# Cross-attention, second phase: steps taken in groups of two, and the next batch's context transposed two groups at a time

## The reference

```
q = (layernorm(x) @ w_q)          # [2, 16 heads, 256, 64]
k = (ctx @ w_k); v = (ctx @ w_v)  # [2, 16 heads, 4096, 64]
attn = softmax(q @ k^T * 64**-0.5)
x = x + (attn @ v) @ w_o
```

## Time and profile before

| | |
|---|---|
| median of 3 runs | 1409.45 us (1409.3 to 1412.59) |
| the profiled execution | 1410.72 us, span 1409.0 us |
| busy | PE 1292.7 us (92%), PEld 1004.9, DVE 868.2, ACT 882.1, POOL 407.6 |
| cross-attention | ends near 1140 us; self-attention and feed-forward take the rest |
| granted TensorE clock, mean | 0.967 of full speed |

### The profile page before, as it was taken

How to read it: one execution, slowest core, us unless ns; L and a number is a source line. 1 busy time by engine, 2 the same in 40 slices (tenths; PEclk the granted TensorE clock), 3 DMA queues, 4 the chain that set the end, 5 groups by cost and what they waited for, 6 DMA issues and landing times. The chain is left out here.

```text
span 1409.0 us, 22447 instructions
## 1 busy us (share of the span) xinstructions
PE 1292.7 (92%) x8447; PEld 1004.9 (71%) x8447; DVE 868.2 (62%) x1121; ACT 882.1 (63%) x1543; POOL 407.6 (29%) x373
## 2 busy tenths in 40 slices
PE   4999999999999999899999999999999969898663
PEld 3887787878787878687878687878787834567423
DVE  4547565657666666655657566666656655657365
ACT  4858585858676776575858586767777512434242
POOL 4505051515243342140515142333324111030000
PEclk9999999999999999999999999999999989998876
DMA  5000000000000001200000000000000053443000
GB/s 167 1 2 20 1 20 1 20 1 20 1 20 16 1 20 45 77 20 2 19 1 20 2 20 1 20 19 2 16 1 5 1 189 55 47 58 42 1 0 15
DMA packets 29685, 34.67 MB, mean 25 GB/s; under 512 B 3984, under 2 KB 26000, under 8 KB 29328
## 3 DMA queue, kind: packets, MB, share of 16 engines
q1 hardware_dynamic: 27536, 29.83, 8.1%
q0 software_dynamic: 2048, 3.43, 1.7%
HBM read 25.89 MB, written 0.52 MB: 19 GB/s over the span
## 5 line engine op out<-in xcount | busy, mean ns | idle before, releaser
L484 DVE TENSOR_TENSOR prob_sum<-prob_sum,probs 128x1024 f32<-128x1024 f32 x224 | 264.7, 1223 | 163.7 <-ACT probs L405 163.0
L320 POOL TENSOR_TENSOR k_split<-probs,k_split 64x512 fp32r<-64x512 f32 x128 | 164.6, 1286 | 358.8 <-ACT probs L367 358.5
L405 ACT ACTIVATE probs<-scores_a 128x1024 f32<-128x1024 f32 x128 | 131.2, 1025 | 191.7 <-PE scores_a L599 191.0
L461 DVE TENSOR_REDUCE step_max<-scores_a 128x2 f32<-128x1024 f32 x128 | 156.6, 1224 | 96.7 <-PE scores_a L587 96.7
L322 POOL TENSOR_TENSOR k_split<-probs,k_split 64x512 fp32r<-64x512 f32 x128 | 164.5, 1285 | 9.6
L461 DVE TENSOR_REDUCE step_max<-scores_b 128x2 f32<-128x1024 f32 x128 | 155.6, 1216 | 0.0
L598 PE MATMUL scores_a<-q_twice,k_split 128*128 128x256 f32 x512 | 139.1, 305 | 4.5 <-ACT q_low_max L394 3.3
L312 POOL TENSOR_TENSOR w_lo<-w_raw,w_hi 128x768 fp32r<-128x768 f32 x16 | 34.9, 2178 | 339.4 <-ACT w_hi L334 339.4
L405 ACT ACTIVATE probs<-scores_b 128x1024 f32<-128x1024 f32 x128 | 131.3, 1026 | 0.0
L598 PE MATMUL scores_b<-q_twice,k_split 128*128 128x256 f32 x512 | 128.4, 283 | 0.0
L599 PE MATMUL scores_b<-q_low_max,k_ones 128*128 128x256 f32 x512 | 127.9, 282 | 0.0
(11 more groups left out here) (213 smaller groups left out, 2605.7 us busy)
## 6 DMA issues: line engine op xcount, KB each, us to landing
ctx_rows<-in_ctx_dram SPq DMA_DIRECT2D x10, 512.0 KB, 3.7
w_raw<-in_L_xattn_w_v_dram SPq DMA_DIRECT2D x14, 256.0 KB, 3.1
probs<-in_ctx_dram SPq DMA_DIRECT2D x6, 512.0 KB, 6.5
grouped<-dots_sb SPq DMA_DIRECT2D x16, 136.0 KB
grouped<-dots_sb POOLq DMA_DIRECT2D x16, 136.0 KB, 13.1
w_raw<-in_L_xattn_w_q_dram SPq DMA_DIRECT2D x16, 128.0 KB, 2.3
w_raw<-in_L_xattn_w_k_dram SPq DMA_DIRECT2D x16, 128.0 KB, 2.4
wo_pair<-in_L_xattn_w_o_dram SPq DMA_DIRECT2D x16, 128.0 KB, 2.1
```

What stands on the lines that cost most here:

```text
L320: pool.tensor_tensor(k_split[DH:P, A, keys], staged[0:DH], k_split[0:DH, A, keys].bitcast(F32), ALU.subtract).then_inc(k_low, 1)
L405: act.activation(probs[:, j % 2, h, :], flat_scores[h], ACT.Exp, scale=SCALE).then_inc(exp_done, 1)
L461: dve.tensor_reduce(step_max[:, :, 1 - h, j - 1], scores[h][:, :, :], X, ALU.max).then_inc(max_done, 1)
L484: dve.tensor_tensor(prob_sum[:, h, :], prob_sum[:, h, :], probs[:, j % 2, h, :], ALU.add).then_inc(sum_done, 1)
```

## The change

On TensorE the eight steps of the second phase are taken in four groups of two: scores of steps 0 and 1, products of 0 and 1, scores of 2 and 3, products of 2 and 3, and so on. The next pair's queries and first keys still stand between the last two products. `next_groups` replaces `next_group`: the groups of the next batch's context are handled two at a time, after the products of steps 1, 3, 5 and 7, on TensorE, ScalarE and VectorE. Buffers, semaphores, DMAs and the number and kind of instructions stay.

```
-        def next_group(b, i, j):
-
-
-            last_pair = isinstance(i, int) and i == PAIRS - 1 and b < BATCH - 1
-            return (b + 1) * LOADS + j - 1 if last_pair and j > 0 else None
+        def next_groups(b, i, j):
+
+            if j % 2 == 0 or stays_in_batch(i) or b == BATCH - 1:
+                return []
+            return [(b + 1) * LOADS + j - 1, (b + 1) * LOADS + j]
...
-                    if next_group(b, i, j) is not None:
-                        context_high(act, next_group(b, i, j))
+                    for n in next_groups(b, i, j):
+                        context_high(act, n)
...
-                if next_group(b, i, STEPS) is not None:
-                    context_high(act, next_group(b, i, STEPS))
...
-                    if next_group(b, i, j) is not None:
-                        context_low(dve, next_group(b, i, j))
+                    for n in next_groups(b, i, j):
+                        context_low(dve, n)
...
-                if next_group(b, i, STEPS) is not None:
-                    context_low(dve, next_group(b, i, STEPS))
...
-                for j in range(STEPS):
-                    for h in (A, B):
-                        scores_by_keys(it, j, h)
-                    if j == 0:
-
-                        project_v(it, b, i, parity, STEPS - 1, tiles=1)
-                    if j > 0:
-                        product_with_v(it, b, i, parity, j - 1)
-                    if next_group(b, i, j) is not None:
-                        transpose_context(next_group(b, i, j))
-                if stays_in_batch(i):
-                    project_q(it + 1, b)
-                    pe.wait_ge(w_low, it + 2)
-                    project_k(it + 1, 0)
-                product_with_v(it, b, i, parity, STEPS - 1)
-                if next_group(b, i, STEPS) is not None:
-                    transpose_context(next_group(b, i, STEPS))
+                for first in range(0, STEPS, 2):
+                    for j in (first, first + 1):
+                        for h in (A, B):
+                            scores_by_keys(it, j, h)
+                        if j == 0:
+
+                            project_v(it, b, i, parity, STEPS - 1, tiles=1)
+                    product_with_v(it, b, i, parity, first)
+                    if first == STEPS - 2 and stays_in_batch(i):
+                        project_q(it + 1, b)
+                        pe.wait_ge(w_low, it + 2)
+                        project_k(it + 1, 0)
+                    product_with_v(it, b, i, parity, first + 1)
+                    for n in next_groups(b, i, first + 1):
+                        transpose_context(n)
```

## The result

The changed kernel takes 1437.06 us (median of 4 runs, 1434.94 to 1440.24) against 1411.02 for the kernel before (4 runs, the three shown earlier and one more). The ratio is 1.0184, 95% interval 1.0165 to 1.0202: slower by 26 us. Forecast were 1440 us, 1429 to 1452. The profiled execution took 1434.94 us, span 1433.2 against 1409.0.

What follows compares the result with a forecast made beforehand. TensorE was taken to bound the kernel. Exponential waits +12.6, last pair of batch 0 +14.0 and clock +4 made +30.6 on the profiled 1410.7, 1441.3; the runs' median being 1.3 lower, 1440 us was predicted, range 1429 to 1452.

Steps and rivals of the forecast that it cites:

- The bound: Cross-attention goes at TensorE's pace: busy 1051 of 1075 us from 60 to 1135 us, so gaps in its list are time.
- What the grouping gives: Second phase: a switch from scores to product and back costs 0.35 us; 3 round trips fewer, 1.05 us a pair.
- the rival that took it for everything: Rival 1: exponentials are released in time and saved switches decide, -3.7 us, 1406 us; chance 4%.
- The wait for the exponential: Groups 2 to 4 of 15 pairs: head A's second scores 0.53 us late, net +0.28 a group, +12.6 us in all.
- The sign of being wrong that I had set: First term is wrong if TensorE's idle ahead of `scores_a` is under 0.25 us; about 0.5 us was expected.
- Single conditions in the group: Head B's second scores just in time, second product in time by 0.3 us, no exponential wait in a pair's first group.
- The last pair of batch 0: Paired context transpositions wait for the single buffer's load, 4.93 us start to start, about 4.1 idle: +14.0 us.
- +4 for the clock: Last pair of batch 0: clock halves 2.2 us into each wait for 6.8 us, 1.4 net lost, at three new places.
- the one in which switches decide: Rival 1: exponentials are released in time and saved switches decide, 1406 us, not slower; chance 4%.
- The full clock: Rival 2: the clock stays full in the 4.1 us waits of batch 0's last pair, +26.6, 1436 us; chance 25%.
- The longer low clock: Rival 3: the clock stays down twice as long, over a whole group, +8, 1448 us; chance 13%.

Runs made afterwards that it cites:

- short exponentials: Against the kernel before: groups of two in 15 pairs, exponentials of steps 2, 4 and 6 there covering half their columns; 1397.07 us, 0.991.
- the filled groups: Against the kernel before: groups of two, in 14 pairs with next queries and first keys between the two steps' scores; 1390.83 us, 0.9853.
- the single filling: Against the kernel before: next queries and first keys placed earlier in 14 pairs, steps alternating, only the last two products together; 1405.28 us, 0.9959.
- the matmuls in the wait: Against the changed kernel: 14 unread matmuls between the two transpositions of each context group pair; 1432.96 us, 1.0156 to the kernel before.
- the context groups alone: Against the kernel before: only the last pair of batch 0 as changed, context transposed two groups at a time; 1430.93 us, 1.0147.

## Why the prediction was right

**The bound.** TensorE's list set the pace, as forecast: the time lost is idle time of TensorE, less what the clock and the saved switches put into and take out of its busy time.

**What the grouping gives.** The 0.35 us a round trip held. The short exponentials show it at 0.353 in written-out pairs, the filled groups at 1.42 for four, the single filling at 0.39 for one. The time lost at a switch between the two forms is thus real, and the rival that took it for everything was refuted only by the wait. That it is the tiling, and not something else in which scores and products differ, no run varied.

**The wait for the exponential.** The mechanism was right and showed where it was expected, 46 waits on `scores_a`. Its size was not. Forecast was +0.28 us a group, measured +0.21 in the loop and +0.08 in written-out pairs, 6.7 us over 15 pairs against 12.6. Two numbers made the difference. I took 0.14 us from a release to the matmul behind it, from a place that waits for VectorE; here it is 0.06 in both kinds of pair, 0.08 less in 45 groups: -3.6. And I took the exponential's start, 1.39 us behind the first scores, from a pair in the loop for all pairs. In the 7 written-out ones it is 1.26, 21 groups at 0.13: -2.7. Together 12.6 - 6.3 = 6.3, and 6.7 was measured. The trace of before has the 1.26 in its written-out pairs too (first scores at 1108.43, exponential at 1109.69 in the last pair); reading one of each kind would have shown it. The sign of being wrong that I had set, an idle of under 0.25 us ahead of `scores_a`, is met in part: the view shows 0.29 us in the 24 groups in the loop, but 0.16 in the 21 written-out ones. I had set it against a delay of 0.5 us, and of a delay the view shows 0.16 us less; delays were 0.45 and 0.32. The wait was there in all 45 and decided the sign, and its term was twice too large.

**Single conditions in the group.** Head B's second scores were in time but for one wait of 0.2 us, in the last pair of batch 0, the second product in all groups, and the first group of a pair had no wait, all as forecast.

**The last pair of batch 0.** Forecast +14.0 and +4 for the clock, measured +20.1. The waits are there, 3.7 to 4.0 us, 4.83 to 5.12 start to start (forecast 4.93). The three rounds to groups 10, 12 and 14 were to take 14.0 us and took 15.2, 16.3 and 15.3; the matmuls in the wait show that this excess is the clock. The step held, the term was small by 1 to 2 us. How it came was also other than put: in the three rounds the clock fell 0.9 us behind the wait's end, 3.1 us into the wait and 0.1 us behind its end, and stayed low for 3.4, 6.8 and 3.4 us, not 6.8 each time. Only the fourth fall came as put, 2.2 us into the wait. The loss in slow work was also put too low, since I read 40% from the lengths of rows; by the starts, 3.4 us at half clock cost 1.5 and 1.7 us. Shorter spells and a larger loss in each partly cancelled, so that the term came near is in part luck. Other executions have other spells: with the context groups alone the last pair cost +21.2. Behind group 15, where I had put nothing, another 1.1 us went. As forecast, a slow clock takes the wait for the exponential away: of the three waits on `scores_a` that this pair's groups could have, one is left.

**The sum.** 12.6 + 14.0 + 4 = 30.6 was forecast, 24.2 by the spans and 26 by the medians came: the groups' term 6 too large, the last pair's 2 too small, and by the spans 2.6 us less in unchanged places. That the total lies inside the range owes something to errors that pull against each other, and more to the load's 4.9 us start to start, read from the trace, which carries 13 of the 30 us. Of the rivals, the one in which switches decide fails by the traces above. The full clock fails by the windows; its 1436 us lies nearer to the median than my 1440, by the groups' error. The longer low clock is seen once, at the fourth wait (10.2 us), not in the groups.

## What to carry to other kernels

Before moving a producer's consumer closer, note for each buffer how long its reader has until the next writer comes; here the exponential had ended 1.6 us before it was needed, and the new order leaves 1.0 us of other work behind the scores for an exponential that needs 1.4 (in the loop, from the end of the scores) with its start and release. A grouping that saves switches needs other work in the gaps that it opens: the groups gave +0.7% bare and -1.5% with the next pair's projections between them, 0.4 of which the projections' place gave without groups. And two operations that go through one buffer, with a load between them, want other work between them: side by side they waited 3.7 to 4.0 us here, with one product between them 2.0, with a step's work 0 to 0.7.

## What the hardware did that was not expected

- The order of two waits in ScalarE's list changes when the exponential starts. With the late wait first it starts 1.39 us behind the first scores in the loop and 1.26 in written-out pairs, with the late wait last 1.26 and 1.34. Why is open.
- The granted clock fell for 3.4 us behind each of three waits of only 2.1 us. The length of the wait doesn't decide by itself. At the loop's jump back TensorE waits 1.5 to 2.2 us in every kernel here; behind five of these 22 waits (1.90 to 2.15 us) the clock fell, behind others of up to 2.15 us it stayed up. So I can't say from these traces which wait will cost its clock; what else decides is open.
- Filling the waits with matmuls nobody reads was worth 5.8 us in the three rounds, of which 1.7 were given back later.
- A wait of 0.02 us costs TensorE 0.12: behind each wait for an exponential read here, that one and those of 0.45 and 0.32 us, the first matmul is followed 0.10 us later than the pace.
